# Moving one PSUM copy of the softmax normalisation from ScalarE to VectorE

## The reference

```python
logits = jnp.einsum('bqnh,bknh->bnqk', q, k)
logits = jnp.where(causal[None, None, :, :], logits, -1e+30)
probs = jax.nn.softmax(logits.astype(jnp.float32), axis=-1).astype(v.dtype)
attn = jnp.einsum('bnqk,bknh->bqnh', probs, v)
return jnp.einsum('bqnh,nhd->bqd', attn, wo)
```

## Time and profile before

| | us |
|---|---|
| two timed runs | 6956.79 and 7866.97, median 7411.88 |
| profiled execution | 6972.4 |
| its span, first to last instruction, slowest core (core 5) | 6970.9 |
| spans of the 8 cores | 6901.4 to 6970.9 |

### The profile page before, as it was taken

The page is one execution under the profiler, slowest core; times in us unless marked ns, Lnnn a source line. Parts: engine busy times, 40 slices in busy tenths (PEclk is TensorE's granted clock), DMA queues, the critical chain, the costliest instruction groups (busy, mean ns, idle before and its releaser), DMA issues.

```text
span 6970.9 us, 66231 instructions; the slowest of 8 cores (6901.4 to 6970.9 us)
## 1 busy us (share of the span) xinstructions
PE 6218.1 (89%) x28144; PEld 2700.6 (39%) x28144; DVE 1180.4 (17%) x1369; ACT 1005.2 (14%) x1241; POOL 305.9 (4%) x280
## 2 busy tenths in 40 slices
PE   1878988887654699999999999999999999999999
PEld 1333432222222244444444444444444444444444
DVE  2222101111123111111111111111000222222222
ACT  6101117774013100000000000000000000000000
POOL 0000000000000000000000000000000000000000
PEclk9999999998876799999999999999999999999999
DMA  6143131113432344444444444444444544474444
GB/s 152 31 82 56 44 73 37 41 42 53 94 101 82 49 56 55 55 55 56 62 55 55 55 60 59 55 55 60 59 66 58 148 118 114 110 199 121 116 108 131
DMA packets 738001, 536.17 MB, mean 77 GB/s; under 512 B 531232, under 2 KB 652192, under 8 KB 733616
## 3 DMA queue, kind: packets, MB, share of 16 engines
q0 software_dynamic: 530896, 207.83, 25.6%
q1 hardware_dynamic: 92896, 208.76, 9.4%
q10 hardware_dynamic: 113920, 115.35, 5.2%
HBM read 623.18 MB, written 116.46 MB: 106 GB/s over the span
## 4 chain that ended last, share of the span: by engine, by line
PE 85%; DMA 6%; ACT 4%; DVE 3%; issue 2%; SPq 0%; DVEq 0%; ACTq 0%; POOL 0%; POOLq 0%
PE pB L940 22%; PE pA L923 22%; PE pA L1036 11%; PE pB L1036 11%; DMA xq<-xin 4%; PE pA L408 3%; PE pB L408 3%; PE pB L651 3%; PE pB L659 2%; PE pA L625 2%; PE pA L488 2%; PE pB L488 2%; PE pA L802 1%; DVE t2b L432 1%; ACT sqb L318 1%
## 5 line engine op out<-in xcount | busy, mean ns | idle before, releaser
L940 PE MATMUL pB<-XLNT,w3c 128*128 128x512 bf16 x7040 | 1549.9, 381 | 0.0
L923 PE MATMUL pA<-XLNT,w1c 128*128 128x512 bf16 x7040 | 1539.8, 379 | 0.0
L940 PEld LDWEIGHTS pB<-XLNT,w3c 128*128 128x128 bf16 x7040 | 691.1, 98 | 843.5 <-issue 21.5
L923 PEld LDWEIGHTS pA<-XLNT,w1c 128*128 128x128 bf16 x7040 | 689.6, 98 | 832.7 <-issue 4.0
L1036 PE MATMUL pA<-w2s,aslg 128*128 128x512 bf16 x3520 | 790.8, 381 | 16.9 <-DMA aslg<-AT_sp 9.1
L1036 PE MATMUL pB<-w2s,aslg 128*128 128x512 bf16 x3520 | 785.8, 379 | 0.2 <-DVE Yacc L1048 0.2
L930 ACT ACTIVATE silu<-pA 128x2048 bf16<-128x2048 f32 x110 | 206.5, 1877 | 2819.0 <-PE pA L923 2764.1
L953 DVE TENSOR_TENSOR atmp<-silu,pB 128x2048 bf16<-128x2048 bf16 x88 | 201.3, 2287 | 2174.7 <-PE pB L940 2126.1
L1036 PEld LDWEIGHTS pA<-w2s,aslg 128*128 128x128 bf16 x3520 | 345.3, 98 | 437.2 <-issue 25.9
L1036 PEld LDWEIGHTS pB<-w2s,aslg 128*128 128x128 bf16 x3520 | 344.3, 98 | 415.7 <-issue 0.6
L632 ACT ACTIVATE exp<-pA,EXB 128x512 bf16<-128x512 f32 (+3 forms) x640 | 382.9, 622 | 173.2 <-PE pA L625 165.6
(11 more groups left out here) (118 smaller groups left out, 2618.6 us busy)
## 6 DMA issues: line engine op xcount, KB each, us to landing
aslg<-AT_sp ACTq DMA_DIRECT2D x80, 1408.0 KB, 7.6
AT_sp<-afin SPq DMA_DIRECT2D x110, 512.0 KB, 7.1
w1c<-w POOLq DMA_DIRECT2D x88, 512.0 KB, 6.7
w3c<-w POOLq DMA_DIRECT2D x88, 512.0 KB, 10.2
w2s<-w POOLq DMA_DIRECT2D x16, 2816.0 KB, 20.8
xt<-xin SPq DMA_DIRECT2D x16, 1024.0 KB, 11.3
xq<-xin SPq DMA_DIRECT2D x64, 256.0 KB, 4.7
X_sp<-x2q SPq DMA_DIRECT2D x64, 256.0 KB, 3.6
```

What stands on the lines that cost most here:

```text
L923: emit("tensor", lambda e, db=db, c=c, slot=slot: e.matmul(pA[:, c * 512:(c + 1) * 512], w1c[slot][:, db * 128:(db + 1) * 128], XLNT[:, db ...
L940: emit("tensor", lambda e, db=db, c=c, slot=slot: e.matmul(pB[:, c * 512:(c + 1) * 512], w3c[slot][:, db * 128:(db + 1) * 128], XLNT[:, db ...
```

## The change

The copy of the spread reciprocals from PSUM to `bcs` is emitted for VectorE as a `tensor_copy`, where ScalarE did it as an activation with the function Copy. It raises the semaphore s_v in place of s_s, so the first value matmuls of the next half and the multiply wait for s_v. Its own waits, its place among the emitted instructions, the tiles and their types are as before. It is one of 32 in a core's run. In VectorE's list it stands right ahead of the multiply L586.

```diff
             tbc = p.tokt("s_t")
-            tbcs = emit("scalar", lambda e, bcps_=bcps_: e.activation(
-                bcs[:, :], bcps_[:, 1024:2048], AF.Copy),
-                waits=[tbc, mul_done[(e_ + 1) % 2]], inc="s_s")
+            tbcs = emit("vector", lambda e, bcps_=bcps_: e.tensor_copy(
+                bcs[:, :], bcps_[:, 1024:2048]),
+                waits=[tbc, mul_done[(e_ + 1) % 2]], inc="s_v")
             tbcs_done[e_ % 2] = tbcs
```

## The result

The changed kernel is slower by 0.74%: the ratio of its runs to those of the kernel before is 1.0074, with a 95% interval of 1.0037 to 1.0110. That is "same" by the 2% bound and still clear of no change. It ran at 7018.44 and 7021.92 us in that comparison and at 7006.72 in a later one, where before ran at 6956.79 to 6984.81. The forecast was +2.4 us, 6974.8, with 6943 to 7005 as its range: wrong in size by about 20 times. In most executions of either kernel the four cores of one die, or all eight, run at a lower clock for long stretches and take up to 15% longer, so all times and stage lengths given here are from the other cores, called undisturbed. Three traces of the changed kernel are used.

The account below looks back on a forecast made before the run. TensorE bounds the kernel, busy 89% of the span; only the attention joints could move. 15 x 0.12 + 16 x 0.02 + 0.26 for the last chain gave +2.4 us on 6972.4, so 6974.8, range 6943 to 7005.

Parts of the forecast that it names:

- The copy's price, its start and its release of TensorE: At each joint: VectorE copy takes 1.21 us, starts when ScalarE's did, TensorE answers after 0.15; value matmul 0.19 or 0.10 later.
- the score matmul's gain: Behind the first value matmul: the score matmul follows after 0.40 us, where it took 0.47 and 0.48.
- VectorE's list and the masks: Short joints: the multiply ends at 1355.40 instead of 1355.14; the step 2 mask behind it has 0.46 us spare, costing nothing.
- From there TensorE's order is as before, so these are what a joint costs: After each joint's score matmul nothing more is lost: +0.12 us per short joint, +0.02 per long one.
- the slow stretches of the same length: Sign expected in the profile after: low-clock stretches at the joints stay as long as before.
- The reading of the earlier trace: At both joints the granted clock is 0.56 to 0.58 for 3.8 to 3.9 us after TensorE restarts, 1.00 afterwards.
- The rival of the clock: An added gap holds the low clock longer at joints: one more slow stretch each, +42 us, 7017; 2%.
- ScalarE's 32.8 us: Rival: TensorE waits at each joint for ScalarE's whole queue, so all the copies' time comes back: 6939.6 us; 5%.
- two elements a cycle: Rival: the VectorE copy runs at double rate, 0.75 us at most, giving -2.8 us, 6969.6; 2%.
- the slow copy: Rival: the VectorE copy takes 1.07 us longer (2.29), delaying value matmuls and masks: +33 us, 7008; 5%.

Follow-up runs that it names:

- dve_halves: Changed kernel with the VectorE copy in two 512-column halves, each first value matmul waiting for its own half; first to last score matmul 650.3 to 656.1 us.
- pe_pad: Kernel before, plus one 128-column broadcast matmul on TensorE ahead of each chain's two; first to last score matmul 664.0 to 667.1 us.

## Why the prediction was wrong, step by step

- **The copy's price, its start and its release of TensorE:** right, within 0.03 us, as was the score matmul's gain. The shortest heads of the changed kernel are 41.02 to 41.06 us: 0.06 to 0.10 over before, where the sum had 0.14 for a short and a long joint. The direct cost is thus, by estimate, some 15 x 0.08 = 1.2 us.
- **VectorE's list and the masks:** right. With a longer list, dve_halves loses nothing.
- **"From there TensorE's order is as before, so these are what a joint costs":** this step failed. The order is as before, the clock isn't. A joint after the change costs what its low stretches make of it, and those went from 3.42 us in nearly every joint to 6.82 in most: 23 to 27 longer stretches per core in place of 0 to 6, at 1.43 us each 30 us, where the sum had 2.4. Two heads of core 7 above are longer by 3.4 and 3.2 us, with two joints each; the direct delay of 0.1 is a thirtieth. The sign "the slow stretches of the same length" failed with it.
- **The reading of the earlier trace rows:** the prediction read a clock of 0.56 to 0.58 for 3.8 to 3.9 us after TensorE starts again. These are means over stretches that were cut at round times. The clock is 0.50 for 3.42 us, and it falls 0.55 us after TensorE has started again in the short joint. That the fall comes behind the restart, and by how little, was in the trace and is what the delay changed.
- **The rival of the clock** had the mechanism and, with one more low stretch per joint, 42 us and 7017, near the measured 7018 and 7022. That the numbers meet is in part luck: the added stretches come in two joints of three and cost 1.43 us each, which makes 30. It got 2%, because the gap added was small "beside a stall of 3.33 that each joint has already". That weighed the wrong thing. In these runs the loss turned not on how much idle time was added but on where the joint stood when the clock fell (1.58 us behind L572 gave 3.41 us of low clock, 1.52 gave 6.82); and that the joints of before all stood at one place, which the prediction took as leave to work with one of each kind, was the warning. Joints that agree to 0.01 us over 400 us of the stage, with the same low stretch each, can be in step with something, and a small edit can end that.
- **The other rivals:** ScalarE's 32.8 us did not come back; the copy did not run two elements a cycle; and the slow copy, whose 7008 lies near the measured 7006.72, took 1.225 us and not 2.29, so that nearness is chance.
- **The range** ended at 7005 and left out the clock; with the stage's 30 us in it, it would have had to reach about 7020.

The Trainium skill ("TensorE: Matmul & The Clock Gate", section "HAM oscillation — how this bites in real kernels") describes a loop in which each tile's wait costs a new fall of the clock. The rows agree: 31 falls in the 31 joints of core 5 of before. Its advice is to arrange the loop so that TensorE stays warm, that is, at the high clock; the run with the stall filled agrees, 1.00 throughout and a stage some 23 us shorter.

The theory that the loss lies elsewhere is out as well. From the last score matmul to the end of the program, the undisturbed cores of before take 5231 to 5297 us and those of the changed kernel 5240 to 5292, with means of 5273 and 5266: the stages behind the attention are not longer.

What stays open: the traces put 25 to 39 us of the loss into this stage, and the slowest core of an undisturbed die loses 31 in the median, while the ratio of whole executions, 1.0074, is some 50. It rests on two of the changed kernel. The core spans narrow this down: in those two and the one of 7006.72 us the mean of the eight cores is 6975, against 6945 in eleven of before, again 30 us. The other 20 lie in how far the slowest core stands above that mean, 31 to 54 us where before has 21 to 39, and whether that is more than chance three executions can't tell. Nor was it shown why 40.96 us holds the joints, only that it does, and that 0.06 us more doesn't. It is not the length of the work in a head: before, the halved copy and 12 filling matmuls have different work and all spend heads at 40.96, and without low stretches a head takes 39.71. It is the distance of the falls from head to head, in before and in pe_pad's first heads alike.

## What to carry to other kernels

Where a loop's period is the same to a few hundredths of a microsecond on all cores, and the granted clock dips at the same place in each pass, compare the starts of the dips with the period before costing a small edit: here delays of up to about 0.1 us a joint cost six to twenty-five times themselves. Two things cured it in these runs: taking the delay off TensorE again (the copy in halves), which gives back the stage of before, and filling the stall of 3.3 us, which gives more. Shortening the stall was not tried. A fill that left 0.73 us of it halved the number of dips, and one that left 0.09 removed them.

## What the hardware showed that I had not expected

- The low stretches of the clock in this stage are 3.4 or 6.8 us long, now and then 10.2, and which of the first two a joint gets turned on 0.1 us of its position (pe_pad: 1.58 or 1.52 us behind L572).
- The same chain of heads (43.7, 44.0, 44.2, 43.7, 43.9, 43.1, 41.3, 41.05 us) came on core 0 in the second and in the third trace of the changed kernel, at different heads: the loss is no noise, it is a course that the loop runs through.
- A PSUM copy on VectorE, f32 to bf16, took 1.225 us for 1024 columns and 0.686 for 512, that is 1.05 ns for each further column; the two-operand multiply of 1024 columns took 1.225 as well, and the copy on ScalarE 1.024. The Trainium skill ("VectorE: DVE Perf Modes", section "The TRN2 errata") gives an estimated 1.19 us for the copy on VectorE, 3% below the measured time.
